# Transposed one-hot matrices of a graph kernel: built by transposes on TensorE, or from a broadcast transfer and a compare in place

## The reference

```
ZU = einsum('nd,kdr->knr', Z, U)
zs, zd = ZU[:, src, :], ZU[:, dst, :]
logits = (zs * zd).sum(-1) / sqrt(R)
exp_l = exp(logits - segment_max(logits, dst)[:, dst])
alpha = exp_l / (segment_sum(exp_l, dst)[:, dst] + 1e-16)
agg = segment_sum(alpha[..., None] * zs, dst)
ssa = einsum('k,knr,kdr->nd', softmax(head_w), agg, U)
Z_half = (1 - C) * Z + C * ssa
... relu of a gradient step with Dmat, then layer norm
```

## Time and profile before

| | us |
|---|---|
| median of 3 runs | 3666.26 |
| lowest and highest | 3658.27 to 3674.17 |
| profiled execution, time | 3677.74 |
| profiled execution, span of the trace | 3675.2 |
| busy: TensorE matmul / weight loads | 1971.2 / 1490.8 |
| busy: VectorE / ScalarE / GpSimd | 1919.5 / 1168.6 / 1728.5 |
| mean granted TensorE clock | 0.577 |

### The profile page before, as it was taken

The page is one execution under the profiler, slowest core; times in us unless marked ns, Lnnn a source line. Parts: engine busy times, 40 slices in busy tenths (PEclk is TensorE's granted clock), DMA queues, the critical chain, the costliest instruction groups (busy, mean ns, idle before and its releaser), DMA issues. The chain is left out here.

```text
span 3675.2 us, 61713 instructions
## 1 busy us (share of the span) xinstructions
PE 1971.2 (54%) x15251; PEld 1490.8 (41%) x15252; DVE 1919.5 (52%) x5864; ACT 1168.6 (32%) x3040; POOL 1728.5 (47%) x1832
## 2 busy tenths in 40 slices
PE   9345545454545445454545455464545454567776
PEld 9233333343434334343424243343433333444666
DVE  4444646454545546454545455464545454666477
ACT  1112323222232323322232233233232322334477
POOL 1544454445444444554544544445544444252662
PEclk7555555555555555555555555555555555577798
DMA  6212222121212212121212112121212121285343
GB/s 205 52 32 46 47 44 46 42 46 42 48 41 47 46 41 48 42 49 40 47 39 48 42 44 48 41 50 41 48 40 45 41 49 39 58 274 179 112 140 107
DMA packets 406593, 232.96 MB, mean 63 GB/s; under 512 B 284096, under 2 KB 371434, under 8 KB 406506
## 3 DMA queue, kind: packets, MB, share of 16 engines
q1 hardware_dynamic: 346666, 154.11, 15.4%
q0 software_dynamic: 59840, 77.87, 9.8%
HBM read 134.80 MB, written 42.55 MB: 48 GB/s over the span
## 5 line engine op out<-in xcount | busy, mean ns | idle before, releaser
L576 POOL DMA_INDIRECT arena<-z_table,sslot x1563 | 1492.0, 955 | 1646.2 <-SPq L418 1114.0
L1347 PE MATMUL bank<-arena 128*128 x4992 | 613.8, 222 | 637.7 <-issue 585.8
L1347 PEld LDWEIGHTS bank<-arena 128*128 128x128 bf16 x4992 | 457.5, 105 | 789.5 <-issue 697.0
L1584 ACT ACTIVATE arena<-bank 128x272 f32<-128x272 f32 x416 | 269.8, 661 | 1574.8 <-remote 970.4
L902 DVE TENSOR_TENSOR xin<-arena,bank 128x512 f32<-128x512 f32 x208 | 143.1, 688 | 1044.3 <-remote 588.2
L1561 ACT ACTIVATE acc<-xTb 128x68 f32 x1600 | 384.6, 312 | 306.6 <-issue 296.0
L1364 PE MATMUL bank<-xto,arena 128*128 128x68 bf16 x3328 | 321.6, 246 | 147.5 <-issue 147.4
L1335 PE MATMUL bank<-ident_b,arena 128*128 128x128 bf16 x1664 | 214.8, 310 | 339.4 <-remote 205.3
L1364 PE MATMUL bank<-arena 128*128 128x68 bf16 x1664 | 296.9, 243 | 120.2 <-issue 90.5
L1364 PEld LDWEIGHTS bank<-xto,arena 128*128 128x128 bf16 x3328 | 281.5, 132 | 166.9 <-issue 166.9
L1335 PEld LDWEIGHTS bank<-ident_b,arena 128*128 128x128 bf16 x1664 | 160.4, 141 | 399.6 <-remote 200.2
(11 more groups left out here) (264 smaller groups left out, 2543.6 us busy)
## 6 DMA issues: line engine op xcount, KB each, us to landing
arena<-arena SPq DMA_DIRECT2D x1660, 32.0 KB
arena<-z_table,sslot POOLq DMA_INDIRECT x1563
dspace<-in_xT SPq DMA_DIRECT2D x49, 256.0 KB
xmz_table<-agn SPq DMA_DIRECT2D x49, 256.0 KB
xmz_table<-arena SPq DMA_DIRECT2D x14, 896.0 KB
arena<-in_x SPq DMA_DIRECT2D x13, 896.0 KB, 11.4
out<-arena SPq DMA_DIRECT2D x12, 896.0 KB
xin<-in_xT SPq DMA_DIRECT2D x8, 896.0 KB
```

Source lines behind the costliest of these rows:

```text
L576: pool.indirect_dma_start(ring[:, e % RING, :], None, z_table, bass.IndirectOffsetOnAxis(ap=sslot[:, e:e + 1], axis=0)).then_inc(tiles_in[ ...
L1347: last = T.matmul(zd_ps[g % 2][:, u * KR:(u + 1) * KR], onehotT[:, g * G + u, :], z3[:, bass.ds(tiles[u], 1), s, :].rearrange("p a c -> p ...
L1584: A.activation(sums[:, :, 1 + q * Q:1 + (q + 1) * Q].rearrange("p c j -> p j c"), sum_ps[q % 2][:, 0:Q * AW].rearrange("p (j c) -> p j c", ...
```

## The change

The transposes and their copies go. At the start the places of all edges (`dloc`, as bf16) are written once to DRAM as `place_rows`. For each block one transfer spreads its 32 rows of 128 places over all 128 partitions, straight into `onehotT` (bf16, 8 KB to a partition, 1 MB in all). VectorE then compares in place with the number of the partition (`make_onehotT`: one small compare for `first_col`, four of 128x1024), right behind `x_ready` and ahead of `scan_steps`. `load_places(b)` stands in SyncE's `turn` between copy groups 0 and 1 and waits until the expansions of the block before have been done (`zd_ready`).

With the transposes' two banks free, `zd_ps` has four banks, one for each group: an expansion waits for the product of the same group one block earlier. `multiply_x` writes bank 3, and the wait for its copy moves from ahead of expand 1 to ahead of expand 3. SyncE loads the eight counts of a block at once (`load_needs`) instead of two in each copy step, and has a `nop` behind the wait for `x_ready`. ScalarE waits before every NSPARE-th (fourth) store of states instead of before each.

```diff
+            def load_places(b):
+                if not (type(b) is int and b == 0):
+                    sp.wait_ge(zd_ready, NG * b)
+                    sp.nop(nofuse=True)
+                sp.dma_start(onehotT.rearrange("p j e -> p (j e)"),
+                             spread(place_rows[bass.ds(b * B, B), :].rearrange("(a j) e -> a (j e)", a=1), 0, P)).then_inc(places_in, 16)
...
+            def load_needs(b):
+                _, need = nc.values_load_multi_w_load_instructions(
+                    needs[0:1, bass.ds(b * NG * 2, 2 * NG)], engines=[mybir.EngineType.SP], min_val=16 * G, max_val=16 * G * EG)
+                return need
...
-                    need = [sp.value_load(needs[0:1, bass.ds((b * NG + g) * 2 + i, 1)], min_val=16 * G, max_val=16 * G * EG) for i in range(2)]
                     for i in range(2):
-                        sp.wait_ge(tiles_in[i], need[i])
+                        sp.wait_ge(tiles_in[i], need[2 * g + i])
...
             def turn(b, h, uses, store, load):
-                for g in range(2):
-                    copy_steps(b, h, g, uses)
+                need = load_needs(b)
+                copy_steps(b, h, 0, uses, need)
+                load_places(b)
+                copy_steps(b, h, 1, uses, need)
                 sp.wait_ge(x_ready, b - 1)
+                sp.nop(nofuse=True)
...
+            dve.wait_ge(tab_ps, 1)
+            V.tensor_copy(place[:, :, :], dloc[:, :, :]).then_inc(place_ready, 1)
...
+            def make_onehotT(b, h):
+                dve.wait_ge(places_in, 16 * (b + 1))
+                V.tensor_scalar(first_col[:, h:h + 1], onehotT[:, 0, 0:1], pno[:, 0:1], None, ALU.is_equal).then_inc(v_step, 1)
+                dve.wait_ge(v_step, vn.next())
+                for g in range(NG):
+                    part = onehotT[:, g * G:(g + 1) * G, :].rearrange("p j e -> p (j e)")
+                    V.tensor_scalar(part, part, pno[:, 0:1], None, ALU.is_equal).then_inc(oneT_ready, 1)
...
                 V.tensor_tensor(xexp, mid_ps[:, 0:P], rev, ALU.subtract).then_inc(x_ready, 1)
+                if more:
+                    make_onehotT(b + 1, 1 - h)
...
             def expand(b, g):
-                if g >= 2 or not (type(b) is int and b == 0):
-                    pe.wait_ge(zd_used, NG * b + g - 1)
+                if not (type(b) is int and b == 0):
+                    pe.wait_ge(zd_used, NG * (b - 1) + g + 1)
...
-                    if u >= NSPARE:
-                        act.wait_ge(state_stored, B * b + u - NSPARE + 1)
+                    if u >= NSPARE and u % NSPARE == 0:
+                        act.wait_ge(state_stored, B * b + u)
```

More of the change, by code:

```diff
@@ L169, in program @@
         srcf_flat = oflat[:, 2 * S:3 * S]
+        place = oflat[:, 2 * S:2 * S + S // 2].bitcast(BF16).rearrange("p (g e) -> p g e", e=P)
         dloc = oflat[:, 3 * S:4 * S].rearrange("p (g e) -> p g e", e=P)
@@ L308, in program @@
         same = same_row.rearrange("p (c j) -> p c j", c=CH)
-        tr_ps = [p[:, :].bitcast(BF16) for p in psum[2:4]]
-        zd_ps = psum[4:6]
+        zd_ps = psum[2:6]
         mid_ps, row_ps = psum[6], psum[7]
@@ L442, in copy_steps @@
                     landed(1 - h, NG - 1, uses - 1 if h == 0 else uses)
+            sp.wait_ge(place_ready, 1)
+            sp.dma_start(place_rows.rearrange("(g p) e -> p g e", p=P), place[:, :, :]).then_inc(places_out, 16)
             sp.wait_ge(moves_ready, 1)
             sp.wait_ge(dloc_ready, 1)
+            need = load_needs(0)
             for g in range(2):
-                copy_steps(0, 0, g, 1)
+                copy_steps(0, 0, g, 1, need)
             sp.wait_ge(reset_ready, 1)
@@ L795, in _ @@
             dve.wait_ge(iotas, 3)
+            dve.wait_ge(places_out, 16)
             V.tensor_copy(spare, arow)
@@ L892, in make_onehot @@
                 for j in range(g * G, (g + 1) * G):
-                    last = V.tensor_scalar(onehot[:, h, j, :], iota_b[:, :], didx[:, h, j:j + 1], None, ALU.is_equal)
-                last.then_inc(onehot_ready, 1)
+                    V.tensor_scalar(onehot[:, h, j, :], iota_b[:, :], didx[:, h, j:j + 1], None, ALU.is_equal)
+            def make_onehotT(b, h):
[5 more added lines that the diff above has]
+                    V.tensor_scalar(part, part, pno[:, 0:1], None, ALU.is_equal).then_inc(oneT_ready, 1)
             def head_products(b, h, g, uses):
@@ L1055, in period @@
                 dve.wait_ge(v_step, vn.next())
+            make_onehotT(0, 0)
             copy_indices(0, 0)
@@ L1368, in period @@
             def period(b, h, xe_uses=None, more=True, dense=True):
-                def next_transposes(g):
-                    if more:
-                        transpose_onehots(b + 1, 1 - h, g)
                 def multiply_x(t):
                     for c in range(DC):
-                        last = T.matmul(zd_ps[1][:, t * D:(t + 1) * D], xe[:, 1 - h, c, t * P:(t + 1) * P], mz[:, c, :],
+                        last = T.matmul(zd_ps[NG - 1][:, t * D:(t + 1) * D], xe[:, 1 - h, c, t * P:(t + 1) * P], mz[:, c, :],
                                         start=(c == 0), stop=(c == DC - 1))
@@ L1422, in period @@
                 if more:
+                    if dense:
+                        pe.wait_ge(xmz_copied, b)
                     expand(b + 1, 3)
                 add_up(b, h, 6, 8)
-            for g in range(NG):
-                transpose_onehots(0, 0, g)
             pe.wait_ge(z_rest, 4)
@@ L1557, in store_states @@
                 for u in range(g * G, (g + 1) * G):
-                    if u >= NSPARE:
-                        act.wait_ge(state_stored, B * b + u - NSPARE + 1)
+                    if u >= NSPARE and u % NSPARE == 0:
+                        act.wait_ge(state_stored, B * b + u)
                     A.activation(acc[:, bass.ds(tiles[u % G], 1), :].rearrange("p a c -> p (a c)"), state[:, :, 1 + u], ACT.Copy
                                  ).then_inc(state_stored, 1)
[L1564 to L1570, removed]
-                A.activation(onehotT[:, g * G:(g + 1) * G, :].rearrange("p j e -> p (j e)"), tr_ps[g % 2][:, :], ACT.Copy).then_inc(oneT_ready, 1)
             def copy_keeps(b):
@@ L1608, in period @@
                 A.activation(ratio[0:1, 1, :], ratio[0:1, 0, :], ACT.Exp, scale=float(R) ** -0.5).then_inc(ratio_ready, 1)
-                if more:
-                    copy_onehots(b + 1, 1 - h, 3)
                 if dense:
@@ L1624, in _ @@
             act.wait_ge(tab_read, 8)
-            for g in range(NG):
-                copy_onehots(0, 0, g)
             period(0, 0, dense=False)
```

45 lines of the change are left out of this document (16 added, 29 removed).

## The result

| | before | changed |
|---|---|---|
| median, us | 3670.22 | 3902.99 (4 runs, 3890.66 to 3914.34) |
| ratio, 95% interval | | 1.0625 [1.0561, 1.0689] |
| span of the profiled execution, us | 3675.2 | 3912.5 |

The forecast was 3618 us, range 3440 to 3800. The time lies outside it, on the other side.

The account below looks back on a forecast made before the run. No engine's busy time bounds the kernel, but gather bursts that slow every instruction stream. C 1.8 us earlier, 0.55 kept, gives 1.0 us per block, times 46, with the start −48: 3618 us after scaling to the median, range 3440 to 3800.

Parts of the forecast that it names:

- What bounds the kernel: Three gather bursts a block, A (8), B (8), C (16); from about 4 us in, all instruction streams are slow.
- SyncE's loads, A to B: Between bursts A and B: eight load records fewer, one transfer issue more; −1.0 us, bounds −1.5 and 0, none reaching C.
- Rival S2: Rival: bursts A and B merge, since SyncE's step comes earlier; +5.1 us a block, 3900 us, chance 0.09.
- B to C: SyncE's way from burst B to burst C, eight load records fewer: −1.5 us, bounds 0 and −3.5.
- C to the end: Of each us that burst C starts earlier, 0.55 us shortens the block: 1.8 us gives 1.0 us per block.
- S1: Rival: burst C catches more of TensorE's work, which then runs slowly; +3 us a block, about 3800 us, chance 0.22.
- C to next A: SyncE between burst C and the next A, one new load against two old: −0.4 to +0.4 us, taken as 0.
- Transposes and ScalarE's copies: Their removal from the path to `x_ready`: −0.3 us, bounds 0 and −6.
- F2: Rival: burst A no longer catches TensorE, `x_ready` up to 6 us sooner, at T+11; about 3440 us, chance 0.14.
- Compares: VectorE's in-place compares before `scan_steps`: 2.3 us in all, covered by TensorE's late add; cost 0, bounds 0 and +0.8.
- S3: Rival: compares hold GpSimd's gathers up at the start of burst B; +2 us a block, 3750 us, chance 0.05.
- Transfer: 1 MB of places into SBUF per block, 12.7 us, landing by T+17 at the latest, when first needed; cost 0.

Follow-up runs that it names:

- the old loads: The changed kernel with SyncE loading its two counts again in each of the four copy steps: 3646.71 us, ratio to the kernel before 0.9858.

## Why the prediction was wrong

- *What bounds the kernel*: right. The slow stretch from about 4 us into a burst was read from the earlier trace rows, and removing it takes 14% off the time. It isn't always 4 us: on SyncE, records stand 0.7 us apart from 2 us behind A's first gather in block 23 before, from 3.7 us behind it in block 26 with the change. But I took the stretch as given, and it was the lever.
- *SyncE's loads, A to B* is the step that failed. The −1.0 us had the right sign and was too small (group 1's first copy came 1.9 us sooner behind A: 0.8 for 2.7). Then I let it vanish: "`x_ready` stands between B and the steps that release C". That put the way from B's earlier start to `x_ready` at nothing, and there the loss arose: `x_ready` at T+25.2 instead of T+17.3. A copy takes 0.65 us where SyncE isn't slowed. In block 26 with the change the first four copies of group 1 go at that pace before SyncE crawls, and four do in the median block; before the change the median block had one. That is the difference between a last copy at A+11.9 and one at A+9.7. The sum treated as smooth what is a threshold: B's first gather 11.8 or 12.3 us behind A's.
- *Rival S2* was the case that came, at 0.09, and its price was near: +5.1 us a block, 3900 us, from block 17; measured +7.1 for a typical block, 4.6 in the mean, 3903. That it was so near is luck, for I misread block 17. Its burst began with a single gather at T+5.5 and went on only at T+8.7, so `x_ready` came early, at T+11.2; the time was lost behind it, where the first add came 24.0 us later instead of 13.0. Block 43 before the change is nearer to what came: its burst of 16 begins at T+2.7, `x_ready` comes at T+25.7 and the block takes 66.2 us. GpSimd's rows there (T is 2735.71) at which a burst begins or pauses, and VectorE's row that signals `x_ready`:

```profile
2738.45 0.95 POOL L576 DMA_INDIRECT arena<-z_table,sslot  x1 [9.32 <-SPq L418]
2741.64 0.95 POOL L576 DMA_INDIRECT arena<-z_table,sslot  x1 [2.24 <-issue]
...
2761.13 0.29 DVE L1012 TENSOR_TENSOR xin<-bank,xin 128x128 f32<-128x128 f32 x1
...
2775.26 0.94 POOL L576 DMA_INDIRECT arena<-z_table,sslot  x1 [15.14 <-SPq L418]
```

  I spoke against S2 with the transfer that is added on the way. Before group 1 it does cost SyncE its issue, 0.38 us at 1832.50, but 8 records went and the start of the whole group moved towards A.
- *B to C*: −1.5 predicted, bounds 0 and −3.5; −5.5 measured. Much of it comes without the merger: in blocks 23, 35 and 39 of the changed kernel, where the bursts aren't run together and `x_ready` comes at T+15.6 to T+16.6, C follows 14.2 to 14.8 us behind it, 3.2 to 3.8 sooner than the 18.0 before. The rest comes with the merged blocks, where B no longer lies beside SyncE's records.
- *C to the end*: I kept 0.55 of an earlier C, by block 25. That block can't give such a rate: it has 24 gathers and no burst B (its A is at T+4.4, and the next gather is C's at T+32.4). C came 5.5 us earlier behind `x_ready`, and the rest of the block grew by 4.6. Nearly nothing was kept. It is what S1 said (39 matmuls more than 4 us into C became 94), as a companion of S2.
- *C to next A*: 0 predicted; from C to group 0's first copy are 23.1 and 23.8 us. Right. A stands earlier behind T only since T itself comes later behind C.
- *Transposes and ScalarE's copies*: −0.3 predicted; with the old loads `x_ready` came 1.2 us sooner, within the bounds. F2 didn't happen.
- *Compares*: right. Four took 1.67 us in block 26, `first_col` 0.20. One takes 0.48 us in the median of 208, and in a run of four they start 0.4 us apart. With the old loads the first add stands at 12.5 behind `x_ready` against 13.0, so they are hidden. By the Trainium skill, VectorE: DVE Perf Modes, The perf-mode tier table, my estimate was 0.4 for one; the trace agrees with it for the distance in a run, and one alone is 0.08 longer.
- *S3*: in the changed kernel the compares mostly run when no gather does, as in block 26, and gathers took 959 ns in the mean against 955. With the old loads the two meet: 64 of the 1563 gathers lie beside one of these compares. They took 1.07 us in the mean, the longest 1.30, and the others 0.96; a compare took 0.49 us beside a gather and 0.48 without, the longest 0.70. So a compare does hold a gather up, by 0.1 us in the mean and one or two gathers a block, and not by the 2 us of S3. The rule in the Trainium skill, SBUF — State Buffer, Who interferes with whom, has one of the two wait until the other's instruction ends. A hold-up is there, but 0.1 us in the mean is far less than a compare's 0.48, so the trace doesn't bear the rule out in full. One such pair, VectorE and GpSimd with the old loads:

```profile
1950.25 1.67 DVE L932 TENSOR_SCALAR arena<-arena,pno 128x1024 bf16<-128x1024 bf16 x4
1950.74 1.30 POOL L603 DMA_INDIRECT arena<-z_table,sslot  x1 [0.30 <-issue]
```

- *Transfer*: hidden, right. VectorE waited for the places before one of its 52 `first_col` compares only.
- *The sum*: without the merged loads the change gives 0.9858. The forecast for the whole was 0.987. That the two are near is luck: nearly all of the forecast's gain stood on SyncE's loads, which this kernel doesn't have, and on the rate from block 25.

What stays open: which part of the rest brings the 1.4% and whether it is real, what in the chip makes the streams crawl, and whether a spacing between 1.25 and 2.65 us without waits would free them as well; it wasn't tried.

## What to carry to other kernels

Where one engine's bursts slow all others, the time depends on how close they come to each other, and an edit that only removes instructions from the engine that releases them can bring them too close: work out the distance to that point, in us, before adding up savings. Blocks or iterations of one trace that fall on either side of such a point show it before anything is built. A gain of 14% was in a place where no row showed a costly instruction, so when a run of instructions makes its neighbours crawl, first try to break the run with a wait for what it has issued. Test the parts of a change alone: here one harmless-looking part cost 6.2% and the others gained 1.4% or nothing.

## What the runs showed of the hardware

Indirect gathers from GpSimd, one every 1.25 us, slow the instruction streams of all engines, down to 5 matmuls in 13 us; the same gathers in runs of four with a wait of 1.8 us behind them let 114 matmuls through in 13 us. With runs of five `x_ready` comes 2 to 3 us later than with four, with six 3 us, with eight 12 us. A gather takes 2.65 us from one start to the next if each waits for the one before to land. The DMA engines were busy for 0.12 of the time in the slow window and for 0.34 in the fast one, so their load isn't the cause. A gather beside a compare of 128x1024 bf16 on VectorE took 1.07 us in the mean, others 0.96 (kernel with the old loads).
